# GpSimd's nucleus-search corrections in a graph network of four layers: fewer and merged operations per tile

## The chip, the cores and the metric

The kernel runs on one core of one Trainium2 chip. The metric is the time of one execution on the device in microseconds (us). The kernel before takes 3471.04 us, the median of three runs (3469.64 to 3474.25).

## What is computed

The reference takes x (3327 x 256) and an adjacency matrix adj (3327 x 3327) and passes them through four graph layers, each on a layer-normalised, rectified copy of x whose output is added to x. Layer 2 is the one that matters here. It runs two steps, and in each it builds an attention matrix in which every row keeps only its largest probabilities until they sum to 0.9 ("nucleus"):

```python
for s in range(STEPS):                       # STEPS = 2
    logits = (Xa @ W1) @ W2 @ (Xa @ W3).T
    idx = jnp.argsort(-logits, axis=1)
    csum = jnp.cumsum(jax.nn.softmax(vals, axis=1), axis=1)
    k_i = jnp.sum(csum < P_NUC, axis=1) + 1  # P_NUC = 0.9
    masked = jnp.where(keep, logits, -jnp.inf)
    A = jax.nn.softmax(masked, axis=1)
    Xf, Xb, Xa = Rf @ Xf, Rb @ Xb, A @ Xa
    Z = Z + (Xf @ U1[s] + Xb @ U2[s] + Xa @ U3[s])
```

Everything is float32.

## The kernel before

Rows are padded to 26 tiles of 128 (`NT = 26`, `NP = 3328`, `N = 3327`). The program has a front part (layer 0 and the row sums), a first plain layer, the attention part (prefix `att_`), and a last plain layer. The attention part is a software pipeline of rounds, about one round to a tile: tiles 0 to 25 are the first step, tiles 26 to 51 the second, with five rounds between them in which no new tile starts (`LAG = 5`). A tile of 128 rows passes through these stages, each a round or so behind the one before:

- **Scores.** TensorE (PE) computes the 128 x 3328 logits in four pieces (L913), ScalarE (ACT) copies each piece into `E` (L1073) and takes its sum (`musum`). VectorE (DVE) takes the row maximum (`row_max`, L1363), ACT the exponential with its row sum `Zs` (L1078).
- **Aiming, on GpSimd (POOL) and ACT.** The sorted prefix of the reference is replaced by a search for the threshold at which the mass above it is 0.9 of `Zs`. `guess(t)` works out a first threshold from the moments of the row and announces it by the semaphore `aimed[0]`. ACT makes two passes over the 3327 elements with it (L1030: a ReLU sum and a sign sum, semaphore `summed[0]`). `update(t, 0)` turns the two sums into a mass and the next threshold, a Newton step, and announces `aimed[1]`. ACT makes two more passes, and `update(t, 1)` makes a secant step and announces the start point by `bracketed`. Each of the three routines is a chain of small POOL operations on one to four values a partition, grouped in stages: `then(...)` issues its operations and waits for all of them before the next stage is issued. `update` also narrows the bracket `ends`.
- **Search, on DVE.** `find(t)` waits for `bracketed`, and takes three evaluations a tile in the first step and four in the second (`EVALS`), each a 3327-element operation (L1401) and some small ones. Then come one more pass (L1408), one or more turns of a loop of MAX8 and MATCH_REPLACE (L1422, L1432), and the masking of the row (L1448, semaphore `probs_ready`). Of these 3327-element operations L1401, L1408 and L1448 are scalar_tensor_tensor and read two tensors; L1363, L1422 and L1432 read one.
- **Use.** PE transposes the masked row in four pieces (L898), ACT copies each piece (L1069) to `PT`/`adj`, and PE multiplies them with the values (L885). In between PE multiplies the adjacency tiles (`neighbours`, L925), which is the most of its work, and makes the small dense products (L932).

The order on each engine is written out by hand. ACT in round i, for k = 0: the copies of k = 0, the exponential of the tile F, then the first pass `sums(R, 1, 0)` of the older tile R, which waits for `aimed[1]` of R; for k = 1: copies and `sums(R, 1, 1)`; for k = 2: copies and `sums(F, 0, 0)`, which waits for `aimed[0]` of F; for k = 3: copies and `sums(F, 0, 1)`. POOL in round i: (second step: sums of layer 2's outputs and layer-norm statistics), `guess(F)`, `update(R, 1)`, the rest of the statistics (`ln_tail`) or two additions of 128 x 256 (L1330, L1334, first step), then `update(F, 0)`. So what POOL announces last in one round, `aimed[1]`, is what ACT waits for near the beginning of the next.

```python
def offer(t, j):
    then(ts(negp[:, t % 2, j:j + 1], cand[:, t % 2, 0:1], -UNDER, None, ALU.mult))
    pool.sem_inc(aimed[j], 1)
```

The functions of the attention part that matter are `offer` (L1196), `prepare` (L1200), `guess` (L1207) and `update` (L1240), which the change rewrites, and on the other engines `sums` (L1020, ACT), `find` and `row_max` (DVE).

## Time and profile before

| | before |
|---|---|
| median of three runs | 3471.04 us (3469.64 to 3474.25) |
| profiled execution: its time, its span | 3468.18 us, 3466.4 us |
| granted TensorE clock, mean | 0.959 |
| PE busy | 3137.2 us (91%), 13212 matmuls |
| DVE busy | 2444.9 us (71%) |
| ACT busy | 1598.2 us (46%) |
| POOL busy | 2140.7 us (62%), 4214 instructions |

Times are microseconds from the start of the span. The clock column of the windows is the share of full speed that was granted to TensorE. The first attention step lies at about 820 to 1850 us, the second at about 1885 to 3210 us. A POOL operation is listed as busy from its start to its end, so time in which it is held up inside counts as busy. "<- issue" or "<- POOLq" behind a wait of ACT on L1030 means that no finished operation of another engine accounts for the end of the wait; those passes wait for a semaphore that POOL's queue raises after its last operation.

### The profile page before, as it was taken

Reading aid. Unit: us, or ns where it says so; the run is one execution under the profiler, and the core shown is the slowest. Engines: PE = TensorE matmul, PEld = TensorE weight load, DVE = VectorE, ACT = ScalarE, POOL = GpSimd, SP = SyncE. Lnnn points to the kernel's source line nnn. Section 1 sums busy time; section 2 is a strip of 40 time slices with the busy share of each in tenths; the row PEclk is TensorE's granted clock in tenths of the full one; section 3 lists DMA queues with packets and bytes.
Section 4 is the critical chain, followed back from the end, with each engine's and each line's share of the span. In section 5 each row is a group of like instructions: output and inputs, shape, how many; then the busy total and the mean of one; then the engine's idle time right before and its main releaser. Section 6 shows DMA issues by size and latency. Waiting matters only on the chain. (4 is left out here: it accounts for less than half of the span.)

```text
span 3466.4 us, 42065 instructions
## 1 busy us (share of the span) xinstructions
PE 3137.2 (91%) x13212; PEld 2267.5 (65%) x13212; DVE 2444.9 (71%) x3401; ACT 1598.2 (46%) x2357; POOL 2140.7 (62%) x4214
## 2 busy tenths in 40 slices
PE   4999999997899999999966698988999999996899
PEld 3888778885567777777754255544566566664788
DVE  6840123333998889888884799999988999998000
ACT  2311322225666666666753455655555555552200
POOL 2212422224788888888880677877888788786211
PEclk9999999998899999999988899999999999998899
DMA  7644344433112222222211111211222222223255
GB/s 258 239 146 146 116 156 166 165 129 87 44 54 59 60 64 58 59 60 64 58 33 63 47 57 48 63 44 55 58 82 75 73 85 82 74 83 103 92 202 173
DMA packets 140702, 327.59 MB, mean 95 GB/s; under 512 B 15456, under 2 KB 93664, under 8 KB 129248
## 3 DMA queue, kind: packets, MB, share of 16 engines
q1 hardware_dynamic: 140512, 325.30, 29.5%
q8 instruction: 90, 1.47, 0.2%
q14 instruction: 100, 0.82, 0.1%
HBM read 286.70 MB, written 38.54 MB: 94 GB/s over the span
## 5 line engine op out<-in xcount | busy, mean ns | idle before, releaser
L1030 ACT ACTIVATE junk<-E,negp 128x3327 uint8<-128x3327 f32 x208 | 637.3, 3064 | 142.8 <-issue 112.0
L1401 DVE SCALAR_TENSOR_TENSOR U<-E,trial 128x3327 f32<-128x3327 f32 x182 | 674.7, 3707 | 0.0
L925 PE MATMUL bank<-big,adj 128*128 128x512 f32 x1352 | 611.4, 603 | 11.2 <-ACT t L1056 11.2
L925 PEld LDWEIGHTS bank<-big,adj 128*128 128x128 f32 x1352 | 253.5, 193 | 333.3 <-issue 332.2
L298 PE MATMUL bank<-big,E 128*128 128x256 f32 x1664 | 364.7, 381 | 1.9 <-PEq L58 1.7
L885 PE MATMUL bank<-Hc,PT 128*128 128x256 f32 x1248 | 303.2, 395 | 66.7 <-ACT PT L1069 66.4
L298 PEld LDWEIGHTS bank<-big,E 128*128 128x128 f32 x1664 | 315.0, 191 | 48.3 <-issue 5.4
L885 PE MATMUL bank<-Hc,adj 128*128 128x256 f32 x1456 | 336.3, 383 | 9.4 <-ACT adj L1069 9.4
L1363 DVE TENSOR_REDUCE nmax<-E 128x1 f32<-128x3327 f32 x52 | 187.9, 3614 | 206.2 <-ACT E L1073 206.2
L885 PEld LDWEIGHTS bank<-Hc,PT 128*128 128x128 f32 x1248 | 244.7, 198 | 127.3 <-ACT PT L1069 77.9
L885 PEld LDWEIGHTS bank<-Hc,adj 128*128 128x128 f32 x1456 | 278.3, 192 | 72.1 <-issue 22.5
L925 PE MATMUL bank<-Hc,adj 128*128 128x256 f32 x1352 | 315.0, 384 | 1.0 <-ACT bias L1050 1.0
L925 PEld LDWEIGHTS bank<-Hc,adj 128*128 128x128 f32 x1352 | 254.2, 191 | 79.1 <-issue 48.8
L898 PE MATMUL tr<-ident,E 128*128 128x128 f32 x1352 | 191.1, 282 | 115.7 <-DVE E L1448 115.7
L1422 DVE MAX8 top<-U 128x8 f32<-128x3327 f32 x74 | 268.4, 3627 | 20.2 <-DVE mass L1410 11.7
L358 POOL TENSOR_TENSOR xn<-xt,t 128x256 f32<-128x256 f32 x52 | 37.7, 725 | 378.8 <-ACT t L329 199.8
L1432 DVE MATCH_REPLACE8 U<-mark,U 128x3336 f32<-128x3336 f32 x74 | 267.7, 3618 | 0.0
L898 PEld LDWEIGHTS tr<-ident,E 128*128 128x128 f32 x1352 | 167.2, 146 | 140.9 <-DVE E L1448 120.9
L913 PE MATMUL lg<-K,qt 64*128 64x384 f32 (+1 forms) x832 | 216.1, 598 | 33.6 <-ACT E L1073 25.3
L1069 ACT ACTIVATE adj<-tr 128x1024 f32<-128x1024 f32 x104 | 95.4, 917 | 255.4 <-PE tr L898 255.3
L1073 ACT ACTIVATE E<-lg 128x1024 f32<-128x1024 f32 x208 | 179.3, 862 | 55.0 <-PE lg L913 49.4
L1408 DVE SCALAR_TENSOR_TENSOR U<-E,ends 128x3327 f32<-128x3327 f32 x52 | 194.0, 3730 | 2.2
(248 smaller groups left out, 5729.7 us busy)
## 6 DMA issues: line engine op xcount, KB each, us to landing
adj<-adjT SPq DMA_DIRECT2D x131, 448.0 KB, 3.4
E<-adjT SPq DMA_DIRECT2D x32, 1664.0 KB, 6.9
adj<-adjT SPq DMA_DIRECT2D x104, 384.0 KB, 3.3
adj<-adjT SPq DMA_DIRECT2D x20, 1664.0 KB, 6.9
E<-adjT SPq DMA_DIRECT2D x26, 1216.0 KB, 5.7
xt<-xin SPq DMA_DIRECT2D x52, 128.0 KB, 5.6
xt<-x_d SPq DMA_DIRECT2D x52, 128.0 KB, 5.3
xo_d<-xo SPq DMA_DIRECT2D x26, 256.0 KB, 3.7
```

The source lines that it names most:

```text
L298: last = nc.tensor.matmul(acc[par][:, 0:D], bufs[par][:, j], rhs[:, j], start=(j == j0), stop=(j == NT - 1))
L885: last = mm(axp[:, 0:D], PT[k % 2][:, h, i * P:(i + 1) * P], Hc[:, j], start=(k == 0 and h == 0 and i == 0), stop=(k == SLOTS - 1 and h == ...
L898: last = nc.tensor.transpose(tr[:, h, i * P:(i + 1) * P], E[:, t % DEPTH, c0:c0 + P], ident[:])
L913: last = mm(lg[:, h, 0:w], qt[rows, t % 2], K2[rows, c0:c0 + w], start=True, stop=True)
L925: last = mm(agg[:, 0:w], adj[:, SPAN * (k % 2) + j - AGG[k]], rhs[:, j], start=(j == 0), stop=False)
L1030: go(junk[:, 0:N], E[:, t % DEPTH, 0:N], func, bias=negp[:, t % 2, j:j + 1], scale=1.0, accum_out=acc_[:, t % 2, j:j + 1]).then_inc(summed ...
L1073: go(halves(E[:, L % DEPTH])[:, :, c0:c0 + w], lg[:, :, 0:w], ACT.Copy, accum_out=musum[:, L % 2, k:k + 1]).then_inc(lg_copied, 1)
L1363: V_.tensor_reduce(nmax[:, t % DEPTH:t % DEPTH + 1], E[:, t % DEPTH, 0:N], axis=AX_X, op=ALU.max, negate=True).then_inc(max_ready, 1)
L1401: V_.scalar_tensor_tensor(out=U[:, 0:N], in0=e, scalar=point, in1=e, op0=ALU.is_ge, op1=ALU.mult, accum_out=found))
L1408: V_.scalar_tensor_tensor(out=U[:, 0:N], in0=e, scalar=hi[:, 0:1], in1=e, op0=ALU.is_lt, op1=ALU.mult, accum_out=sc[:, 5:6]))
L1422: rthen(V_.memset(U[:, N:NPAD], 0.0), V_.max(top8[:], U[:, 0:N]))
L1432: V_.match_replace(U[:], mark[:], U[:], MARKED).then_inc(rnd, 1)
```

## The change

All of it is in the three POOL routines and the two helpers that they call.

- `guess`: one operation (L1224) goes, its constant is folded into L1226, which becomes a tensor_scalar with a pointer operand. The three targets of the row (`tgt`, its negative, and `below`) are written by one 3-element tensor_tensor with constants instead of three operations in two stages; `below` is now tgt x (1 - 2^-22) instead of tgt x (1 - 2^-24), up to rounding. The secant terms (L1204, L1205) are no longer made in `guess`, and the pair of sums (L1203, now `aims`) runs beside `ends2` and the slope.
- `update(t, 0)`: the complement of the flag (`took[0]`, `took[2]`) is compared directly, beside the flag. The upper clip moves into the product before it at both places, and the lower clip and the negated threshold are made side by side from the same value. The secant terms are made here, for the second point.
- `update(t, 1)`: the same, and the slope is no longer stored: its factors are multiplied with the gap, in two stages fewer.
- Three constants are added to `known`, `trial2` grows from 5 to 7 columns.

POOL's stream has 4202 instructions in the program before and 3890 after, which is 6 fewer for each of the 52 tiles. No other engine's instructions change in kind or number.

```diff
--- before.py
+++ after.py
@@ -42,7 +42,7 @@
 LATE = 7
 FIRST = 7
 SPAN = 7
-POINT, GAP, GOAL, MASS, BELOW = 0, 1, 2, 3, 4
+POINT, GAP, GOAL, MASS, BELOW, NEG = 0, 1, 2, 3, 4, 6
 
 
 @contextmanager
@@ -655,7 +655,7 @@
             over = ab("over", [P, 2, 2])
             sign = ab("sign", [P, 2, POINTS])
             negp = ab("negp", [P, 2, POINTS])
-            known = ab("known", [P, 8])
+            known = ab("known", [P, 11])
             outset = ab("outset", [P, 2, 2, 2])
             ga = ab("ga", [P, 2, 20])
             up = ab("up", [P, 2, 24])
@@ -663,7 +663,7 @@
             took = ab("took", [P, 3])
             parts = ab("parts", [P, 2, 2, 2])
             ends2 = ab("ends2", [P, DEPTH, 2, 2])
-            trial2 = ab("trial2", [P, DEPTH, 5])
+            trial2 = ab("trial2", [P, DEPTH, 7])
             side = ab("side", [P, 2, 2], I32)
             sc = ab("sc", [P, 8])
             top8 = ab("top8", [P, TOP])
@@ -1171,7 +1171,8 @@
                         G_ = nc.gpsimd
                         tt = G_.tensor_tensor
                         ts = G_.tensor_scalar
-                        KNOWN = (1.0 / ROOT, -1.0, 0.5, float(np.e), AIM[0], STEER[0], AIM[1], STEER[1])
+                        KNOWN = (1.0 / ROOT, -1.0, 0.5, float(np.e), AIM[0], STEER[0], AIM[1], STEER[1],
+                                 P_NUC, P_NUC * (1 - 2.0 ** -22), -P_NUC)
                         values = [(known[:, i:i + 1], value) for i, value in enumerate(KNOWN)]
                         for h, scaled, fixed in ((0, 1 - P_NUC, 0.0), (1, -P_NUC, 1.5)):
                             values += [(outset[:, 0, h, 0:1], 0.0), (outset[:, 0, h, 1:2], scaled),
@@ -1193,23 +1194,16 @@
                             pool.sem_clear(step_done)
                             n[0] = 0
 
-                        def offer(t, j):
-                            then(ts(negp[:, t % 2, j:j + 1], cand[:, t % 2, 0:1], -UNDER, None, ALU.mult))
-                            pool.sem_inc(aimed[j], 1)
-
-                        def prepare(t):
+                        def aims(t):
                             q, step = t % 2, t // NT
-                            p = cand[:, q, 0:1]
-                            then(ts(up[:, q, 0:2], known[:, 4 + 2 * step:6 + 2 * step], p, ga[:, q, 12:13], ALU.mult, ALU.add),
-                                 ts(up[:, q, 3:4], p, p, RIDGE[step] ** 2, ALU.mult, ALU.mult))
-                            then(tt(up[:, q, 4:5], up[:, q, 3:4], ga[:, q, 11:12], ALU.mult))
+                            return ts(up[:, q, 0:2], known[:, 4 + 2 * step:6 + 2 * step], cand[:, q, 0:1],
+                                      trial2[:, t % DEPTH, NEG:NEG + 1], ALU.mult, ALU.add)
 
                         def guess(t):
                             q, d, step = t % 2, t % DEPTH, t // NT
                             ga_ = lambda a: ga[:, q, a:a + 1]
                             restart()
                             z, nm = Zs[:, d:d + 1], nmax[:, d:d + 1]
-                            tgt, below = (trial2[:, d, a:a + 1] for a in (GOAL, BELOW))
                             p = cand[:, q, 0:1]
                             pool.wait_ge(exp_done, t + 1)
                             if t >= DEPTH:
@@ -1220,23 +1214,21 @@
                                  ts(ga_(4), ga_(2), ROOT, -ROOT - math.log(N), ALU.mult, ALU.add))
                             then(ts(ga_(5), ga_(3), 1.0 / N, nm, ALU.mult, ALU.add))
                             then(tt(ga_(6), ga_(4), ga_(5), ALU.subtract))
-                            then(ts(ga_(7), ga_(6), 2.0, 0.01, ALU.mult, ALU.add),
-                                 ts(ga_(8), ga_(5), 1.0, -SHIFT[step], ALU.mult, ALU.add))
+                            then(ts(ga_(7), ga_(6), 2.0, 0.01, ALU.mult, ALU.add))
                             then(tt(ga_(9), ga_(7), half, ALU.pow),
-                                 tt(ga_(10), ga_(8), ga_(7), ALU.add))
+                                 ts(ga_(10), ga_(7), -SHIFT[step], ga_(5), ALU.add, ALU.add))
                             then(ts(ga_(13), ga_(9), -QUANTILE, ga_(10), ALU.mult, ALU.add))
                             then(ts(ga_(14), ga_(13), -0.001, -36.0, ALU.min, ALU.max))
                             then(tt(p, e_, ga_(14), ALU.pow))
-                            offer(t, 0)
+                            then(ts(negp[:, q, 0:1], p, -UNDER, None, ALU.mult))
+                            pool.sem_inc(aimed[0], 1)
                             shape4 = lambda ap: ap.rearrange("p a b -> p (a b)")
                             then(tt(shape4(parts[:, 0]), z.to_broadcast([P, 4]), shape4(outset[:, 0]), ALU.mult),
-                                 ts(tgt, z, P_NUC, None, ALU.mult),
-                                 ts(ga_(12), z, -P_NUC, None, ALU.mult),
+                                 tt(trial2[:, d, GOAL:NEG + 1:2], z.to_broadcast([P, 3]), known[:, 8:11], ALU.mult),
                                  tt(ga_(15), z, minus, ALU.pow))
                             then(tt(ends2[:, d], parts[:, 0], outset[:, 1], ALU.add),
-                                 ts(below, tgt, 1 - 2.0 ** -24, None, ALU.mult),
+                                 aims(t),
                                  ts(ga_(11), ga_(15), ga_(9), 1.0 / DENSITY, ALU.mult, ALU.mult))
-                            prepare(t)
 
                         def update(t, j):
                             q, d, step = t % 2, t % DEPTH, t // NT
@@ -1251,31 +1243,37 @@
                             pool.wait_ge(summed[j], PASSES[j] * (t + 1))
                             then(ts(count, sign[:, q, j:j + 1], 0.5, N / 2, ALU.mult, ALU.add))
                             then(ts(mass_, count, p, over[:, q, j:j + 1], ALU.mult, ALU.add))
-                            then(ts(cand[:, q, 1:3], up[:, q, 0:2], mass_, None, ALU.add),
-                                 ts(took[:, 1:2], mass_, tgt, None, ALU.is_ge))
-                            if j > 0:
-                                then(tt(up_(16), mass_, up_(7 + j), ALU.subtract))
+                            if j == 0:
+                                then(ts(cand[:, q, 1:3], up[:, q, 0:2], mass_, None, ALU.add),
+                                     ts(took[:, 1:2], mass_, tgt, None, ALU.is_ge),
+                                     ts(took[:, 0:3:2], mass_.to_broadcast([P, 2]), tgt, None, ALU.is_lt))
+                                then(ts(up_(21), slip, slope, STRIDE, ALU.mult, ALU.min))
+                            else:
+                                then(ts(cand[:, q, 1:3], up[:, q, 0:2], mass_, None, ALU.add),
+                                     tt(up_(16), up_(7 + j), mass_, ALU.subtract),
+                                     ts(took[:, 1:2], mass_, tgt, None, ALU.is_ge),
+                                     ts(took[:, 0:3:2], mass_.to_broadcast([P, 2]), tgt, None, ALU.is_lt))
                                 then(ts(up_(17), up_(16), up_(16), up_(3), ALU.mult, ALU.add),
-                                     tt(up_(18), up_(16), up_(20), ALU.mult))
+                                     ts(up_(18), up_(16), up_(20), up_(4), ALU.mult, ALU.add))
                                 then(tt(up_(19), up_(17), minus, ALU.pow),
-                                     tt(up_(18), up_(4), up_(18), ALU.subtract))
-                                then(tt(slope, up_(18), up_(19), ALU.mult))
-                            then(tt(up_(21), slip, slope, ALU.mult),
-                                 ts(took[:, 0:3:2], took[:, 1:2].to_broadcast([P, 2]), -1.0, 1.0, ALU.mult, ALU.add))
+                                     tt(up_(22), up_(18), slip, ALU.mult))
+                                then(ts(up_(21), up_(22), up_(19), STRIDE, ALU.mult, ALU.min))
                             wide = lambda ap: ap.unsqueeze(2).to_broadcast([P, 2, 2])
-                            then(ts(up_(20), up_(21), STRIDE, -STRIDE, ALU.min, ALU.max),
+                            then(ts(up_(20), up_(21), -STRIDE, None, ALU.max),
                                  tt(parts[:, 0], ends, wide(took[:, 0:2]), ALU.mult),
                                  tt(parts[:, 1], cand[:, q, 0:2].unsqueeze(1).to_broadcast([P, 2, 2]),
                                     wide(took[:, 1:3]), ALU.mult))
                             then(tt(up_(22), e_, up_(20), ALU.pow),
                                  tt(ends, parts[:, 0], parts[:, 1], ALU.add))
-                            then(tt(up_(23), up_(22), p, ALU.mult))
+                            then(ts(up_(23), up_(22), p, hi, ALU.mult, ALU.min))
                             if j < POINTS - 1:
-                                then(ts(p, up_(23), hi, lo, ALU.min, ALU.max))
-                                offer(t, j + 1)
-                                prepare(t)
+                                then(ts(negp[:, q, j + 1:j + 2], up_(23), lo, -UNDER, ALU.max, ALU.mult),
+                                     ts(p, up_(23), lo, None, ALU.max))
+                                pool.sem_inc(aimed[j + 1], 1)
+                                then(aims(t), ts(up_(3), p, p, RIDGE[step] ** 2, ALU.mult, ALU.mult))
+                                then(tt(up_(4), up_(3), slope, ALU.mult))
                             else:
-                                then(ts(point, up_(23), hi, lo, ALU.min, ALU.max))
+                                then(ts(point, up_(23), lo, None, ALU.max))
                                 pool.sem_inc(bracketed, 1)
 
                         def ln_tail(st, done, sums_, b):
```

The order on POOL at two places of the first step. The end of `guess` for one tile and the begin of the routine behind it, before (`Zs` is the row sum, `ga` and `up` scratch, `trial` holds the targets):

```order
L1232 TENSOR_TENSOR parts<-Zs,outset 128x4
L1233 TENSOR_SCALAR trial<-Zs 128x1
L1234 TENSOR_SCALAR ga<-Zs 128x1
L1235 TENSOR_TENSOR ga<-Zs,known 128x1
L1236 TENSOR_TENSOR ends<-parts,outset 128x4
L1237 TENSOR_SCALAR trial<-trial 128x1
L1238 TENSOR_SCALAR ga<-ga 128x1
L1203 TENSOR_SCALAR up<-known,cand,ga 128x2
L1204 TENSOR_SCALAR up<-cand 128x1
L1205 TENSOR_TENSOR up<-up,ga 128x1
```

and the same place in the changed kernel:

```order
L1226 TENSOR_TENSOR parts<-Zs,outset 128x4
L1227 TENSOR_TENSOR trial<-Zs,known 128x3
L1228 TENSOR_TENSOR ga<-Zs,known 128x1
L1229 TENSOR_TENSOR ends<-parts,outset 128x4
L1199 TENSOR_SCALAR up<-known,cand,trial 128x2
L1231 TENSOR_SCALAR ga<-ga 128x1
```

Ten operations in four stages have become six in two. The second place is `update(t, 0)` from the flag to the threshold that ACT waits for, before:

```order
L1255 TENSOR_SCALAR took<-up,trial 128x1
L1263 TENSOR_TENSOR up<-cand,ga 128x1
L1264 TENSOR_SCALAR took<-took 128x2
L1266 TENSOR_SCALAR up<-up 128x1
L1267 TENSOR_TENSOR parts<-ends,took 128x4
L1268 TENSOR_TENSOR parts<-cand,took 128x4
L1270 TENSOR_TENSOR up<-known,up 128x1
L1271 TENSOR_TENSOR ends<-parts 128x4
L1272 TENSOR_TENSOR up<-up,cand 128x1
L1274 TENSOR_SCALAR cand<-up,ends 128x1
L1197 TENSOR_SCALAR negp<-cand 128x1
```

and after:

```order
L1248 TENSOR_SCALAR took<-up,trial 128x1
L1249 TENSOR_SCALAR took<-up,trial 128x2
L1250 TENSOR_SCALAR up<-cand,ga 128x1
L1262 TENSOR_SCALAR up<-up 128x1
L1263 TENSOR_TENSOR parts<-ends,took 128x4
L1264 TENSOR_TENSOR parts<-cand,took 128x4
L1266 TENSOR_TENSOR up<-known,up 128x1
L1267 TENSOR_TENSOR ends<-parts 128x4
L1268 TENSOR_SCALAR up<-up,cand,ends 128x1
L1270 TENSOR_SCALAR negp<-up,ends 128x1
L1271 TENSOR_SCALAR cand<-up,ends 128x1
```

The number is the same, but L1249 now stands before the stage of L1250, and L1270 and L1271 are one stage instead of two.

## Rows read from the trace of the kernel before

**Rows 1.** Windows, four rounds: length; PE, PEld, DVE, ACT, POOL busy; clock; DMA:

```profile
1242.40:1282.90 40.50, 38.53 (x174) 28.78 (x173) 34.39 (x50) 26.17 (x31) 35.15 (x66) 0.96 0.20 58
1282.90:1319.40 36.50, 36.50 (x173) 27.66 (x172) 34.76 (x57) 26.18 (x31) 30.35 (x63) 1.00 0.22 64
...
1395.00:1439.50 44.50, 39.15 (x173) 29.27 (x172) 36.08 (x53) 26.17 (x31) 37.61 (x74) 0.92 0.19 52
...
1553.80:1592.80 39.00, 36.79 (x173) 27.57 (x173) 34.25 (x50) 25.95 (x31) 34.10 (x63) 1.00 0.21 59
```

**Rows 2.** Waits from 1006 to 1748 us (us in total, times, longest):

```profile
ACT junk L1030 <- issue: 86.6, 14, 9.0
...
PE bank L885 <- ACT PT L1069: 35.3, 14, 5.4
...
POOL up L1252 <- ACT junk L1030: 4.5, 5, 1.6
```

**Rows 3.** The timeline of one round, 1549 to 1570 us (start, duration, operation):

```profile
1549.65 3.62 DVE L1363 TENSOR_REDUCE nmax<-E 128x1 f32<-128x3327 f32 x1 [3.26 <-ACT E L1073]
1552.40 0.19 ACT L1030 ACTIVATION_READ_ACCUMULATOR junk<-E,negp 128x1 f32 x1
1553.37 3.68 DVE L1401 SCALAR_TENSOR_TENSOR U<-E,trial 128x3327 f32<-128x3327 f32 x1
1553.39 4.26 POOL L1334 TENSOR_TENSOR adj<-t,Hc 128x256 f32<-128x256 f32 x1
1557.92 0.19 POOL L1252 TENSOR_SCALAR up<-sign 128x1 f32<-128x1 f32 x1 [0.27 <-POOL adj L1334]
1559.06 3.68 DVE L1401 SCALAR_TENSOR_TENSOR U<-E,trial 128x3327 f32<-128x3327 f32 x1
1559.32 3.46 POOL L1263 TENSOR_TENSOR up<-cand,ga 128x1 f32<-128x1 f32 x1
1564.39 3.68 DVE L1401 SCALAR_TENSOR_TENSOR U<-E,trial 128x3327 f32<-128x3327 f32 x1
1564.42 3.69 POOL L1272 TENSOR_TENSOR up<-up,cand 128x1 f32<-128x1 f32 x1
1568.64 0.25 POOL L1197 TENSOR_SCALAR negp<-cand 128x1 f32<-128x1 f32 x1
1569.03 3.07 ACT L1030 ACTIVATE junk<-E,negp 128x3327 uint8<-128x3327 f32 x1 [5.87 <-issue]
1569.11 3.40 POOL L1203 TENSOR_SCALAR up<-known,cand,ga 128x2 f32<-128x2 f32 x1 [0.22 <-POOL negp L1197]
```

**Rows 4.** The same round's end, POOL and DVE:

```profile
1581.44 3.67 POOL L1205 TENSOR_TENSOR up<-up,ga 128x1 f32<-128x1 f32 x1
1581.45 3.60 DVE L1448 SCALAR_TENSOR_TENSOR E<-U,E 128x3327 f32<-128x3327 f32 x1
```

**Rows 5.** POOL's groups from 1006 to 1748 us (busy, mean ns of one | idle before):

```profile
L1224 POOL TENSOR_SCALAR ga<-ga 128x1 f32<-128x1 f32 x19 | 3.6, 191 | 1.6
L1233 POOL TENSOR_SCALAR trial<-Zs 128x1 f32<-128x1 f32 x19 | 3.9, 208 | 1.6
L1238 POOL TENSOR_SCALAR ga<-ga 128x1 f32<-128x1 f32 x19 | 4.9, 260 | 2.0
L1258 POOL TENSOR_SCALAR up<-up 128x1 f32<-128x1 f32 x19 | 6.4, 334 | 2.1
```

**Rows 6.** Waits from 1748 to 1885 us, the end of the first step:

```profile
PE bank L885 <- ACT PT L1069: 24.9, 4, 14.9
...
DVE sc L1399 <- POOLq L1279: 6.6, 2, 6.2
```

**Rows 7.** The second step: waits 1950 to 2480 us and 2400 to 2530 us, window 2524.7 to 3067.8 us:

```profile
PE tr L898 <- DVE E L1448: 74.4, 7, 26.3
...
PE bank L925 <- ACT t L1056: 8.6, 1, 8.6
...
2524.70:3067.80 543.10, 538.66 (x2003) 333.06 (x2002) 508.62 (x754) 311.55 (x429) 446.29 (x839) 1.00 0.27 79
```

## Prediction, written before the changed kernel ran

> **What bounds the kernel now.** I read the busy shares first, then the windows round by round, then who waits for whom, and last the timeline of one round. POOL is busy 62% of the span and PE 91%, so by the shares a change on POOL alone should be worth nothing. The windows say otherwise for the first attention step. A round in which PE never idles takes 36.5 us; the other rounds take 39.0, 40.5 and 44.5 us, and PE idles 2.0 to 5.4 us of each [rows 1]. The waits name the cause: PE waits 14 times, 35.3 us in all, for the copy L1069 on ACT; ACT, which works in order, was itself held 14 times, 86.6 us in all, before its pass L1030, by nothing that has a row, and that is the semaphore `aimed[1]` from POOL's queue. POOL waits for ACT only 4.5 us in the same 742 us [rows 2]. So in this step POOL's chain is the loop that sets the round, about 39.0 us against PE's 36.5.
>
> The timeline shows why 60 operations a tile fill 39 us. POOL's L1334, which is one addition, starts 0.02 us behind DVE's L1401 and lasts until that has ended. L1263 and L1272 do the same behind the next two L1401, and L1203 is held 3.4 us by L1408 [rows 3]; L1205 lasts the 3.6 us of L1448 [rows 4]. Beside L1363 POOL runs on. So in each tile five 3.6 to 3.7 us operations of DVE hold POOL up, with one operation caught in each, and POOL works only in what is left: some 1.6 us between two L1401, the time beside L1363, and that beside L1422 and L1432. The caught operations last 3.4 to 4.3 us, where small ones that run free last 0.19 to 0.33 [rows 3, 5].
>
> The second step is different. From 2525 to 3068 us PE is busy 538.7 of 543.1 us, so nothing on POOL can help there. Before it, from 1950 to 2480 us, PE waits 74.4 us for L1448, the end of DVE's own search, which is bound by DVE's passes; one wait of 8.6 us at about 2480 is for ACT behind POOL's statistics [rows 7].
>
> **The change, part by part**, as free-running POOL time for one tile. A tensor_tensor or a tensor_scalar with constants costs 0.19 us, with one pointer 0.26, with two 0.33 [rows 5], and a stage's end about 0.1 more.
> - `guess` loses L1224 (0.19), L1233 and L1234 (0.21 each) for one 3-element operation (0.2), L1237 (0.21), L1204 (0.26) and L1205 (0.19); L1226 gets a pointer (+0.07). That is 1.27 - 0.27 = 1.0 us, and two stages less, 1.2 us. `aimed[0]` comes only 0.1 us sooner after the start of `guess`.
> - `update(t, 1)` loses one operation and two stages, but four of the rest become operations with pointers. The durations come out even, the stages give 0.2 us.
> - `update(t, 0)` keeps its 17 operations. It gains the second flag, wider clips and the secant terms' place; it loses one stage. I take 0, with bounds of 0.3 us either way (one operation with pointers).
> - Three memsets once: nothing. DVE, ACT and PE keep their instructions; `trial2`'s wider rows change no size.
> Together 1.4 us of some 22 us free-running POOL work in a 39 us round.
>
> **What a round becomes.** I carry the timeline of [rows 3] over to PE's own pace and count from the start of L1363. PE stops being delayed if the wait of ACT is short enough: ACT waited 5.87 us there [rows 3] and PE idled 2.2 in that round (39.00 less 36.79) [rows 1], so 3.7 us are covered by PE's other work. `aimed[1]` may come up to 17.2 us after L1363 starts; it came at 19.2. DVE keeps its pace: L1401 at 3.7, 9.4 and 14.7 us, the first gap being 0.4 us longer than the second because L1334 was in flight.
> - Before, `guess` ends just as L1448 starts, so L1205 is caught (L1205 at 1581.44) [rows 4], `update(t, 1)` starts after it, the two additions run into L1401, and `update(t, 0)` starts at 8.3 us, in the gap behind it. Its fourteen operations to `aimed[1]` then need two more gaps, and L1272 misses the third L1401 by 0.03 us [rows 3].
> - After, `guess` is done 1.2 us sooner, so three or four operations of `update(t, 1)` pass before L1448. By the stage costs above `bracketed` then comes at about 1 us instead of 2.9, the additions end at 2.5, and `update(t, 0)` can start at 3.1, as soon as ACT's pass is read (1552.59) [rows 3]. Two stages pass before the first L1401; from its end at 7.4 the flags take to 8.0, the step to 8.3, the bracket's parts to 8.9; the power falls on the second L1401 and ends by 13.2; product, clip and offer need 1.0 to 1.2 us more, so `aimed[1]` comes at about 14.4. The third L1401 starts at 14.4. Either it is passed, or the offer is caught and comes at 18.3.
> - If it is passed, ACT waits under 1 us and PE does not wait. POOL's `update(t, 1)` of the next tile ends again at about 1 us of the next round, so the state holds itself up.
>
> **The sum.** First step, 1006 to 1748 us: of 35.3 us I let one long wait of 5 stay, -30. Two of the rounds with gaps show a granted clock of 0.96 and 0.92 and 38.5 and 39.2 us busy, where rounds without a gap have 1.00 and 36.5 [rows 1]; with the gaps most of that goes too, -3. End of the step: PE's 24.9 us and DVE's 6.6 us of waits are the latency of the last tiles [rows 6]; POOL gets there earlier within its round, -3, from bounds of 0 and -7. Second step: the 8.6 us wait may fall by one caught operation (3.6), or others may be caught instead; -1, from bounds of -7 and +6. Sum -37 us of the profiled execution's 3468.2, 3431; the median of the runs stands 2.9 above that execution, so 3434. I set 3436 for the likeliest case, since the long waits of the transition (44.5 us round) may come twice.
>
> A rule of the Trainium skill bears on this, and can be left out of what stands above. SBUF — State Buffer, section "Who interferes with whom", says that a VectorE instruction with two SBUF inputs contends with GpSimd's reads, that the later one blocks fully, and that issue order decides. By that rule the caught operations cost the rest of the pass, and a chain that is a little shorter can gain a whole pass of 3.7 us or nothing; a shared bandwidth would give only 1.4 us a round. The rows agree with the rule; it also says that a reduction never contends, as beside L1363.
>
> **The rivals.**
> - *Throughput only.* The offer stays behind the third L1401 in most rounds, since two operations now stand in its stage and both must be done. Then 1.4 us less work is worth at most 1.0 to 1.4 us in each of 14 gapped rounds, and 2 to 3 in the long ones: 14 x 1.2 = 17, with 3 for the rest -20, 3448 in the profile, 3451 in the median. For it: the margin at 14.4 us is nil by my estimates. Against it: a caught offer gives POOL a longer round (37.7 us), and with that a head start in the next.
> - *The gain is taken by DVE.* DVE's tile is 35.4 us from the start of L1363 to the end of L1448 [rows 3, 4], PE's 36.5, and a tile with another turn of the loop of L1422 and L1432 takes longer. If PE's gaps become waits for L1448, half of the 30 stays: 3449.
> - *Nothing.* The waits of ACT are of another origin than POOL's chain length, or the second step gives it all back: 3468 to 3474. Little speaks for it, as POOL itself waits only 4.5 us.
> - *Slower.* The pair of flags with pointers before the Newton step, and the two-operation offer, put `update(t, 0)` one pass of DVE further back: the chain starts a stage before an L1401 rather than behind it, so that five stages instead of four lie in each gap. Then a round is like that of 44.5 us with its gap of 5.4 us [rows 1], +3.4 us on each. It decides if `aimed[1]` is later than 21 us after L1363 starts, and needs more than four such rounds to outweigh the rest; with eight of the 19 it is +27 - 10 = +17, 3488.
>
> **How the numbers follow.** Forecast (gaps mostly closed) 0.55, 3420 to 3446. Throughput only 0.2, gain taken by DVE 0.12, both 3443 to 3458. Nothing 0.07. Slower 0.06. The range 3420 to 3459 leaves out the last two and a little of the first. A measurement of this kernel can tell 0.2%, about 7 us, from no change: the first three cases are faster by more than that, 0.87; of "nothing" all is within, 0.07; slower 0.06.
>
> **What would show it.** In the profile after: 312 POOL instructions fewer; the wait of PE on L1069's copies between 1006 us and the end of the first step under 10 us; rounds of 36.5 us; the wait of ACT before L1030 mostly under 1 us; `update(t, 0)` starting before the first L1401 and its offer ending before the third; the first step over 30 to 40 us earlier. From 2525 us on the rounds stay at 49.3 us (543.1 over eleven), and the second step's length stays within 6 us of before. The forecast is wrong if ACT's wait is still over 4 us in most rounds, if PE waits for L1448 instead, or if the second step is longer by what the first gives.

## The result, and the profile after

The changed kernel is slower. Its median is 3511.02 us (3477.27 to 3512.76, 13 runs) beside 3471.68 us (3468.77 to 3474.26, 13 runs) before: a ratio of 1.0092, 95% interval 1.007 to 1.0114. The forecast was 3436 us, the range 3420 to 3459. Its runs don't scatter about one value as those of before do: most lie at 3510 to 3513, others at 3477, 3496 and 3502. The profiled execution is one of 3477.27 us, so its profile shows 9.1 us of a loss of 39.

| | before | after, the execution of 3477 us |
|---|---|---|
| span | 3466.4 us | 3475.5 us |
| POOL busy, instructions | 2140.7 us, 4214 | 2146.1 us, 3905 |
| first step, 19 rounds | 1006.2 to 1747.6 us | 1009.5 to 1752.4 us |
| the next two stretches of PE's rhythm (end of the step) | 210.5 us | 212.0 us |
| from there to the end | 1508.3 us | 1511.1 us |

Of these 9.1 us only 1.5 lie in the 19 rounds, 3.3 ahead of them, 1.5 at the end of the step and 2.8 behind it. POOL has 309 operations fewer and is no less busy. The waits from 1006 to 1748 us, in the columns of [rows 2]:

```profile
ACT junk L1030 <- issue: 95.8, 18, 11.7
DVE nmax L1361 <- ACT E L1073: 62.9, 15, 9.9
...
PE bank L885 <- ACT PT L1069: 37.4, 15, 8.0
...
POOL up L1244 <- ACT junk L1030: 19.8, 4, 5.7
```

PE's wait was to fall from 35.3 us to under 10; it is 37.4, and ACT waits 18 times instead of 14. Four windows of rounds, in the columns of [rows 1]:

```profile
1208.60:1246.80 38.20, 36.85 (x174) 27.61 (x173) 33.88 (x50) 26.00 (x32) 33.96 (x57) 1.00 0.22 61
1246.80:1285.00 38.20, 36.85 (x174) 27.64 (x173) 33.86 (x50) 26.00 (x32) 33.96 (x57) 1.00 0.22 61
1398.00:1445.20 47.20, 39.18 (x174) 29.26 (x173) 36.12 (x51) 26.28 (x32) 38.49 (x69) 0.89 0.17 50
1445.20:1481.70 36.50, 36.50 (x174) 27.63 (x173) 33.80 (x50) 26.14 (x32) 31.18 (x51) 1.00 0.22 63
```

The steady round did get shorter, 38.2 us instead of 39.0. But three rounds take 45 to 47 us, each beside one of 36.5; before there were two of 44.5. One steady round, 1207 to 1232 us, against [rows 3]:

```profile
1208.32 3.62 DVE L1361 TENSOR_REDUCE nmax<-E 128x1 f32<-128x3327 f32 x1 [3.25 <-ACT E L1073]
...
1212.05 3.68 DVE L1399 SCALAR_TENSOR_TENSOR U<-E,trial 128x3327 f32<-128x3327 f32 x1
1217.38 3.68 DVE L1399 SCALAR_TENSOR_TENSOR U<-E,trial 128x3327 f32<-128x3327 f32 x1
1222.66 3.68 DVE L1399 SCALAR_TENSOR_TENSOR U<-E,trial 128x3327 f32<-128x3327 f32 x1
```

```profile
1210.92 0.73 POOL L1332 TENSOR_TENSOR adj<-t,Hc 128x256 f32<-128x256 f32 x1
1211.93 0.19 POOL L1244 TENSOR_SCALAR up<-sign 128x1 f32<-128x1 f32 x1 [0.28 <-POOL adj L1332]
1212.22 3.72 POOL L1245 TENSOR_SCALAR up<-up,cand,over 128x1 f32<-128x1 f32 x1
1216.04 0.30 POOL L1247 TENSOR_SCALAR cand<-up 128x2 f32<-128x2 f32 x1
...
1217.53 3.58 POOL L1263 TENSOR_TENSOR parts<-ends,took 128x4 f32<-128x4 f32 x1
...
1222.18 0.38 POOL L1268 TENSOR_SCALAR up<-up,cand,ends 128x1 f32<-128x1 f32 x1
1222.65 3.77 POOL L1270 TENSOR_SCALAR negp<-up,ends 128x1 f32<-128x1 f32 x1
1226.40 0.31 POOL L1271 TENSOR_SCALAR cand<-up,ends 128x1 f32<-128x1 f32 x1
```

(U is the tile that L1399 writes; "caught" means held until a pass of DVE has ended.) As forecast, the two additions end before the first pass over U (L1332 at 1211.65), but `update(t, 0)` starts 3.6 us after L1361's start and not 3.1. The offer L1270 starts 0.01 us ahead of the third pass, is caught, and comes at 18.1 us after L1361's start instead of 14.4. The second step did what was forecast: from 1950 to 2480 us PE waits 73.1 us for L1446 (before 74.4), and the 543 us window is as full.

```profile
PE tr L898 <- DVE E L1446: 73.1, 7, 26.2
...
2531.00:3074.00 543.00, 538.10 (x2002) 332.78 (x2001) 507.71 (x757) 309.96 (x430) 452.73 (x770) 1.00 0.27 79
```

### The profile page after: what moved, and what is told of

The parts are those of the page before. It is cut to its first block and busy times, and to the rows that moved or that the text cites. A ratio compares the mean times of both kernels' runs of the same rounds, so it can differ in the third digit from the quotient of the medians.

```text
span 3475.5 us, 41756 instructions
## 1 busy us (share of the span) xinstructions
PE 3144.0 (90%) x13212; PEld 2273.9 (65%) x13212; DVE 2440.9 (70%) x3401; ACT 1598.5 (46%) x2357; POOL 2146.1 (62%) x3905
## 5 line engine op out<-in xcount | busy, mean ns | idle before, releaser
L1399 DVE SCALAR_TENSOR_TENSOR U<-E,trial 128x3327 f32<-128x3327 f32 x182 | 672.5, 3695 | 0.0
L1361 DVE TENSOR_REDUCE nmax<-E 128x1 f32<-128x3327 f32 x52 | 188.0, 3615 | 217.0 <-ACT E L1073 217.0
L1406 DVE SCALAR_TENSOR_TENSOR U<-E,ends 128x3327 f32<-128x3327 f32 x52 | 193.1, 3714 | 2.2
```

Of the source, the lines that this page charges most:

```text
L1361: V_.tensor_reduce(nmax[:, t % DEPTH:t % DEPTH + 1], E[:, t % DEPTH, 0:N], axis=AX_X, op=ALU.max, negate=True).then_inc(max_ready, 1)
L1399: V_.scalar_tensor_tensor(out=U[:, 0:N], in0=e, scalar=point, in1=e, op0=ALU.is_ge, op1=ALU.mult, accum_out=found))
L1406: V_.scalar_tensor_tensor(out=U[:, 0:N], in0=e, scalar=hi[:, 0:1], in1=e, op0=ALU.is_lt, op1=ALU.mult, accum_out=sc[:, 5:6]))
```

## The experiments

Each kernel was timed beside the kernel before on the same chip, whose medians were 3467.7 to 3470.4 us. "Offer" is the end of `negp` for the second candidate, timed from the start of DVE's row maximum (in the changed text the announcement waits for L1271 too, 0.3 us more, or a whole pass where L1271 is caught); "passes" are the three over U (L1401, after: L1399) and the one behind them (L1408, after: L1406).

**The parts of the change.** First the changed kernel again (e1), then its `guess` in the old kernel (e2: the hunks of the diff up to `update`, with `then(aims(t), ts(up_(3), ...))` in place of `prepare(t)`), its `update` with the old `guess` (e3), and the changed kernel with the second flag made from the first (e4):

```diff
-                                     ts(took[:, 1:2], mass_, tgt, None, ALU.is_ge),
-                                     ts(took[:, 0:3:2], mass_.to_broadcast([P, 2]), tgt, None, ALU.is_lt))
-                                then(ts(up_(21), slip, slope, STRIDE, ALU.mult, ALU.min))
+                                     ts(took[:, 1:2], mass_, tgt, None, ALU.is_ge))
+                                then(ts(up_(21), slip, slope, STRIDE, ALU.mult, ALU.min),
+                                     ts(took[:, 0:3:2], took[:, 1:2].to_broadcast([P, 2]), -1.0, 1.0, ALU.mult, ALU.add))
```

> The changed kernel once more, for a profile of an execution at its usual time (its profiled execution took 3477 us, its median is 3511). Theory A (pass alignment): the rounds of the first step fall into one of two patterns, a steady one of 38.2 us with the offer caught behind the third L1399, and pairs of 45 and 36.5 us in which a chain lags one whole pass of DVE; the usual execution has at least ten pairs' worth of rounds of 45 us where the profiled one had four, and the first step takes all of the 34 us. Theory B (fixed price of the edits): all rounds are equally longer than 38.8 us, or the 34 us lie in the second step.

> Only the edits in guess (19 operations for 24), update as before but for the secant terms that both kernels make for the second point. Theory A: the step is set by where update(t, 0) starts against DVE's passes; with guess 1.2 us shorter and the old update, the offer lands behind the second or third pass, time anywhere from 3430 to 3515 and possibly of two kinds; halves need not add up. Theory B: guess only removes work, so it is faster than before by 10 to 25 us (3447 to 3461), and the loss of the change lies in update.

> Only the edits in update, guess as before with its 24 operations. Theory A: the offer comes 0 to 0.3 us later or sooner than before; before it was caught by 0.03 us, so little changes unless a pass is crossed: 3465 to 3475, or one jump. Theory B: the wide flags and the two-operation offer cost 0.3 us on the path in every round of the first step and lose alignment: 3490 to 3530, more than the whole change.

> The changed kernel with the second flag made as before, from the first, in the stage of the Newton step of update(t, 0) (0.19 us with constants instead of 0.30 with a pointer). Theory A: in the steady pattern the offer missed the third L1399 by 0.01 us, and 0.1 us less on the path lets it pass, so that the wait of PE on L1069 goes to zero in those rounds: under 3460 if the pattern of 45 us rounds is also left, at least 10 us under the changed kernel otherwise. Theory B: the flag is one of several costs: 3 to 8 us less than the changed kernel, 3503 to 3508.

Measured: e1 3478.14 us (3476.12 to 3509.42, 10 runs; ratio 1.0041, 1.0021 to 1.006), e2 **3436.59** (3435.27 to 3437.95; ratio 0.9902, 0.9886 to 0.9919), e3 **3517.95** (3514.85 to 3518.98; 1.0135, 1.0118 to 1.0152), e4 3477.59 (3476.49 to 3480.2, 9 runs). So `guess` alone gives the gain that was forecast for the whole, and `update` alone costs 48 us. The changed kernel itself lost 39 us in the first batch of runs and 8 in this one; its quick runs, two of 13 there, are six of ten here. Why is not shown, so a version of it can be judged against it only within one batch. Of e2 the waits from 1006 to 1748 us and two rounds:

```profile
ACT junk L1030 <- issue: 54.8, 10, 7.1
...
PE bank L885 <- ACT PT L1069: 24.5, 9, 8.6
```

```profile
1464.70:1501.20 36.50, 36.50 (x174) 27.63 (x173) 33.73 (x50) 26.19 (x31) 32.27 (x56) 1.00 0.22 64
1501.20:1539.40 38.20, 36.77 (x173) 27.58 (x172) 33.77 (x50) 25.97 (x31) 33.56 (x60) 1.00 0.21 61
```

Its rounds alternate, the offer coming at 14.4 us in one and at 18.5 in the next. In e3 they alternate between 36.5 and 45.4 to 46 us, with offers at 14.2 and 23.8. e4, whose flag is about 0.1 us cheaper, has e1's median and none of its scatter; at least 10 us less was expected. In its steady rounds the 0.1 us is lost at once: L1263 is caught by the second pass as before, the same operations follow behind it, and L1270 again starts 0.01 us ahead of the third.

**One update at a time, and a dose.** e5 has the new text for `update(t, 0)` alone, e6 for `update(t, 1)` alone. e7 has nothing of the change, but one unused operation:

```diff
                             then(ts(mass_, count, p, over[:, q, j:j + 1], ALU.mult, ALU.add))
+                            if j == 0:
+                                then(ts(up_(12), mass_, 0.5, 1.0, ALU.mult, ALU.add))
```

> The kernel before with the change's text for update(t, 0) alone (two flags with pointers, the step bounded from above in its multiply, product with the upper clip, offer and point in one stage, the secant terms behind the offer); guess and update(t, 1) as before. Theory A (pass alignment): what matters is where update(t, 0) stands in DVE's gaps. Its fourteen-odd operations to the offer were measured 0.33 us longer than before when none was caught, and the offer needs 0.3 more; that should be enough to push a further operation into a pass in every second round, pairs of 36.5 and 45 us as in the version with both updates, 3505 to 3520. Theory B (each edit costs its own duration, whatever the alignment): 19 rounds by 0.6 us is at most 12 us, 3475 to 3483.

> The kernel before with the change's text for update(t, 1) alone; guess and update(t, 0) as before. Measured free-running it is 0.25 us longer. Theory A (pass alignment): it delays the two additions and so the start of update(t, 0) by one quarter of a microsecond, which only counts if the chain of update(t, 0) has no slack left at its third L1401; before it missed that pass by 0.03 us, so most rounds can get no worse by it, 3468 to 3480; if it alone gives the pairs of 45 and 36.5 us, update(t, 1) is the culprit and the time is over 3500. Theory B (own duration): 19 rounds by 0.25 us, 3475.

> The kernel before with one more stage of one operation with constants (0.19 us and a stage's end, 0.28 us together) in update(t, 0), behind its mass; the value is not used. Nothing of the change is in it. Theory A (pass alignment): the same pairs of 36.5 and 45 us as with the change's updates appear from a third of a microsecond of any work, and the time is 3500 to 3520. Theory B (own duration): 19 rounds by 0.28 us, 3475 to 3477. If it stays at 3470 to 3480 the loss of the change's updates is not a matter of their length before the offer.

Measured: e5 3517.75 us (1.0139, 1.0122 to 1.0155), e6 3467.95 (0.9993, 0.9984 to 1.0003; 10 runs), e7 **3514.78** (1.0127, 1.011 to 1.0144). An operation of 0.19 us, which ought to cost 5 us in 19 rounds, costs 45; a quarter of a microsecond in `update(t, 1)` costs nothing. The loss of e3 is that of the new `update(t, 0)` alone. e7's windows:

```profile
1095.80:1132.40 36.60, 36.60 (x174) 27.70 (x174) 33.58 (x49) 26.19 (x31) 32.20 (x60) 1.00 0.22 64
1132.40:1177.70 45.30, 38.57 (x173) 28.87 (x172) 34.93 (x51) 26.20 (x31) 36.36 (x68) 0.92 0.18 51
```

This speaks for pass alignment against a price by duration, and the loss needs no property of the new operations. The new `guess` with only one of the new updates was not run.

**Attempts at the better side, and the dose in the other versions.** e8 is e2 with `update(F, 0)` moved ahead of the two additions (L1330, L1334). e9 and e10 put e7's operation into the changed kernel and into e2. e11 is e2 with the second flag, both bracket products and the bracket's sum behind the offer, so the second candidate is clipped to the old bracket. e12 is one more profiled execution of the changed kernel.

> The kernel before with the change's guess (3436.6 us before) and with POOL's two additions of 128x256 halves moved behind update(t, 0), so that update(t, 0) may start as soon as ACT's first pass is read. Theory A (pass alignment): every second round had its offer caught at 18.5 us after the start of DVE's row maximum; with the additions out of the way update(t, 0) starts 1 to 2 us sooner, one operation fewer stands before the first L1401, the offer passes before the third L1401 at about 14.4 in nearly all rounds, and rounds are 36.5 us: 12 to 17 us less than 3436.6, 3420 to 3426. Against it: whoever waits for the additions (PE's transposes of the next activations) gets them 14 us later; if that is on the path, 3440 or more. Theory B: the order of equal work changes nothing, 3436.

> The changed kernel with the same unused 0.19 us operation as a stage of its own in update(t, 0). Theory A (pass alignment): the changed kernel stands on an edge; in its steady rounds of 38.2 us the offer started 0.01 us ahead of the third pass over U and was caught, coming at 18.1 us after the start of DVE's row maximum. With 0.28 us more it is past the edge, one operation further back, and every second round has its offer at about 23.5: the pattern of pairs 36.5 and 45.4 us all through the step, 3508 to 3520, in every run, where the changed kernel itself gives 3477 in some runs and 3511 in others. Theory B (own duration): 3478 and 19 times 0.28 = 3483.

> The kernel before with the change's guess (3436.6 us before) and with the same unused operation in update(t, 0). Theory A (pass alignment): the offer, which passed ahead of the third pass over U in every second round (14.4 us) and was caught in the others (18.5), is caught in all; rounds of 38.1 us, and perhaps some pairs with 45: 3460 to 3480, about what the changed kernel gives in its quicker runs. So the loss of the change's updates on top of its guess is this edge. Theory B (own duration): 3442.

> The kernel before with the change's guess, and in update(t, 0) the opposite of the added stage: the second flag, the two bracket products and the bracket's sum (four operations, some 0.6 us) come behind the offer. That alters the computation in one point: the second candidate is clipped to the bracket as it was before this update, no longer to the new one. The work in all is the same but for one copy more. Theory A (pass alignment): after the second pass over U some 1.0 us of chain is left up to the offer, and the gap is 1.6 us, so the offer passes ahead of the third pass in every round, comes at about 14.3, ACT waits no more, and nearly all rounds of the step take 36.5 us: 3415 to 3428. Theory B (own duration): the work is not less, 3437 or a little more.

Measured: e8 3435.77 us (0.9897, 0.9881 to 0.9914), no different from e2, where 3420 to 3426 was expected. e9 **3478.75** (3472.81 to 3493.99), where 3508 to 3520 was expected. e10 3458.05 (0.9966, 0.9953 to 0.9979; expected 3460 to 3480), e11 **3445.93** (0.9929, 0.9916 to 0.9943), 9 us slower than e2 where 10 to 20 us less was expected. e12's execution was again one of 3477 us. So 0.28 us costs 45 us in the kernel before and 21 in e2, and a path to the offer that is 0.6 us shorter can lose. e9's median is e1's, but the changed kernel was not timed in e9's batch; its profile shows why it need not lose: the second pass catches one operation earlier, and the offer still comes at 18.2 us. In e11 the offer did pass ahead of the third pass in two rounds of three (14.6 and 13.5 us), later in the step in one of two, but the other round had begun with an addition caught in the first pass, the offer's last operation L1259 fell 0.16 us behind the third, and it came at 19.2. In e2 no addition is caught in its steady rounds: the work moved behind the offer comes ahead of the additions of the next round.

**How fine the edge is.** e13, e14 and e15 read one constant from SBUF, the same value, in the changed kernel, the kernel before and e2; that operation takes 0.26 instead of 0.19 us. e16 is e2 again.

```diff
-                            then(ts(count, sign[:, q, j:j + 1], 0.5, N / 2, ALU.mult, ALU.add))
+                            then(ts(count, sign[:, q, j:j + 1], known[:, 2:3] if j == 0 else 0.5, N / 2, ALU.mult, ALU.add))
```

> The changed kernel with one constant (0.5) of the first operation of update(t, 0) read from SBUF instead, the same value: that operation takes about 0.07 us longer and nothing else is altered. Theory A (pass alignment): the changed kernel stands on an edge of a few hundredths of a microsecond in the rounds that follow a pair of 36.5 and 45 us; pushed over it, it keeps to the pairs, each 5.5 us longer than two rounds of 38.2, and six such pairs make 3477 into 3511. So 3505 to 3515 in most runs, with pairs in the profile in place of the rounds of 38.2. If it lands on another pattern it may be 3473 to 3480, as with the whole added stage. Theory B (own duration): 19 times 0.07, 3479, and the spread of the changed kernel as before.

> The kernel before with the same 0.07 us. A stage more of 0.28 us made it 3514.8. Theory A (pass alignment): the time stands on steps; in the rounds of 39.0 us the bracket's sum already missed the third pass over U by 0.03 us, so 0.07 us more changes no catch there, 3468 to 3474; should one catch change, over 3490; a time between is against it. Theory B (own duration): 3471.

> The kernel before with the change's guess (3436.6 us before) and the same 0.07 us in update(t, 0): how near to an edge this version stands. Theory A (pass alignment): its good rounds have the offer at 14.4 us, right ahead of the third pass over U; if 0.07 us more makes it miss, 3450 to 3460 as with a whole stage more (3458.1), if not 3435 to 3439. Theory B (own duration): 3438.

(The operation called the bracket's sum in e14's text is the product L1272.) Measured: e13 **3508.86** us (3506.54 to 3510.16), e14 **3513.89** (1.0135, 1.0118 to 1.0152), e15 3441.92 (0.9927, 0.9911 to 0.9944), e16 3436.23 (0.991, 0.9894 to 0.9927). 0.07 us makes the kernel before 46 us slower. e15 lies between the two values expected: its rounds are those of e2 (19 take 718.2 us, e2's 718.1), and the end of the step is 5 us longer (213.2 against 207.9). The kernel before in the round of 39.2 us that follows its first pair of 44.4 and 36.5 (row maximum at 1082.94 us), with DVE's passes first and POOL's operations after:

```profile
1086.83 3.67 DVE L1401 SCALAR_TENSOR_TENSOR U<-E,trial 128x3327 f32<-128x3327 f32 x1
...
1092.52 3.68 DVE L1401 SCALAR_TENSOR_TENSOR U<-E,trial 128x3327 f32<-128x3327 f32 x1
...
1097.85 3.68 DVE L1401 SCALAR_TENSOR_TENSOR U<-E,trial 128x3327 f32<-128x3327 f32 x1
...
1102.08 3.68 DVE L1408 SCALAR_TENSOR_TENSOR U<-E,ends 128x3327 f32<-128x3327 f32 x1
```

```profile
1086.97 4.13 POOL L1334 TENSOR_TENSOR adj<-t,Hc 128x256 f32<-128x256 f32 x1
...
1092.41 0.29 POOL L1255 TENSOR_SCALAR took<-up,trial 128x1 f32<-128x1 f32 x1
1092.78 3.46 POOL L1263 TENSOR_TENSOR up<-cand,ga 128x1 f32<-128x1 f32 x1
...
1097.88 3.70 POOL L1272 TENSOR_TENSOR up<-up,cand 128x1 f32<-128x1 f32 x1
1101.69 0.33 POOL L1274 TENSOR_SCALAR cand<-up,ends 128x1 f32<-128x1 f32 x1
1102.10 0.25 POOL L1197 TENSOR_SCALAR negp<-cand 128x1 f32<-128x1 f32 x1
```

And the same place of e14 (row maximum at 1087.73 us), whose passes start at 1091.75, 1097.42, 1102.69 and 1106.89 us:

```profile
1097.42 3.67 DVE L1401 SCALAR_TENSOR_TENSOR U<-E,trial 128x3327 f32<-128x3327 f32 x1
...
1106.89 3.68 DVE L1408 SCALAR_TENSOR_TENSOR U<-E,ends 128x3327 f32<-128x3327 f32 x1
```

```profile
1091.89 4.12 POOL L1334 TENSOR_TENSOR adj<-t,Hc 128x256 f32<-128x256 f32 x1
1096.30 0.26 POOL L1252 TENSOR_SCALAR up<-sign,known 128x1 f32<-128x1 f32 x1 [0.29 <-POOL adj L1334]
...
1097.40 3.78 POOL L1255 TENSOR_SCALAR took<-up,trial 128x1 f32<-128x1 f32 x1
...
1102.84 3.59 POOL L1271 TENSOR_TENSOR ends<-parts 128x4 f32<-128x4 f32 x1
...
1106.82 3.79 POOL L1274 TENSOR_SCALAR cand<-up,ends 128x1 f32<-128x1 f32 x1
1110.69 0.25 POOL L1197 TENSOR_SCALAR negp<-cand 128x1 f32<-128x1 f32 x1
```

Before, L1255 started 0.11 us ahead of the second pass and got through, the clip L1274 fitted ahead of L1408, and the offer L1197 got by it too. With 0.07 us more L1255 starts 0.02 us ahead and is caught; each later catch then falls on an earlier operation, and the clip is caught by the fourth pass too. The offer comes at 23.2 us instead of 19.4, one pass later. e14's text had looked for the edge at the third pass; it lay at the second. In both kernels the round shown begins with an addition caught by the first pass, behind a round of 36.5 us. The kernel before gets away with 39.2 us and goes over to its rounds of about 39.0; e14's takes 45, the next is one of 36.5 again, and behind it an addition is caught again. A pair takes 81.7 us (e14: 36.5 and 45.2) where two rounds of 39.0 take 78. The clock does its part, as e14's long round shows:

```profile
1137.00:1173.40 36.40, 36.40 (x173) 27.55 (x172) 33.63 (x50) 26.19 (x31) 32.05 (x59) 1.00 0.21 63
1173.40:1218.60 45.20, 38.98 (x173) 29.13 (x173) 34.47 (x51) 26.19 (x31) 35.88 (x66) 0.92 0.18 52
```

Behind a gap of 6 us the granted clock is 0.92 in the mean, a mixture of the levels 2.4 and 1.2 GHz, and the same matmuls take 39.0 us instead of 36.5.

**The last link.** In e13's profile the point was ready and not announced:

```profile
1182.15 3.87 POOL L1268 TENSOR_SCALAR up<-up,cand,ends 128x1 f32<-128x1 f32 x1
1186.11 0.30 POOL L1270 TENSOR_SCALAR negp<-up,ends 128x1 f32<-128x1 f32 x1
1186.38 3.73 POOL L1271 TENSOR_SCALAR cand<-up,ends 128x1 f32<-128x1 f32 x1
```

e17 (on e13) and e18 (on the changed kernel) announce behind `negp` alone:

```diff
-                                then(ts(negp[:, q, j + 1:j + 2], up_(23), lo, -UNDER, ALU.max, ALU.mult),
-                                     ts(p, up_(23), lo, None, ALU.max))
+                                then(ts(negp[:, q, j + 1:j + 2], up_(23), lo, -UNDER, ALU.max, ALU.mult))
                                 pool.sem_inc(aimed[j + 1], 1)
+                                then(ts(p, up_(23), lo, None, ALU.max))
```

> The changed kernel with the 0.07 us pointer (3508.9 us), and the offer announced behind negp alone; the other operation of that stage, the new p, becomes a stage of its own behind the announcement. In the profile with the pointer, negp was done at 1186.41 us but p started at 1186.38, 0.03 us behind DVE's pass L1406, and was caught for 3.73 us, so ACT was released at 1190.2. Theory A (pass alignment): announced alone the offer is 3.8 us earlier in each of these rounds, ACT waits about 5.5 instead of 9.3, PE's gap of 5.6 us falls to about 2, and the pairs of 36.5 and 45.3 go over into others: 3465 to 3485. Theory B (own duration): one stage more behind the offer, 3509 to 3511.

> The changed kernel with the offer announced behind negp alone. Theory A (pass alignment): in its steady rounds negp itself is caught and done at 1226.42 us and p at 1226.71, so the offer gains only 0.3 us there; rounds of 37.9 us instead of 38.2, and the pairs at 1055 and 1401 us, where negp is caught by L1406 itself, stay: 3470 to 3477; the runs of 3496 and 3511 us are gone, because these hang on p being caught. Theory B (own duration): 3478 to 3480, with the spread of before.

Measured: e17 3505.86 us (1.0101, 1.0084 to 1.0118), e18 **3506.76** (3504.44 to 3512.05; 1.0102, 1.0085 to 1.0119). Both expectations missed: announcing earlier gave neither version the gain expected (e13 stood at 3508.9). Whether e18 loses against the changed kernel is open, as that was not timed in this batch: e18's runs are 28 us above e1's median and 4 under the 3511 of the first batch. Its profile shows the pattern of nine pairs. In e18 the one stage more behind the offer puts `update(t, 1)` one operation back at L1446 against the changed kernel's quick profile (L1255 is caught where it was L1256), so in every second round the addition L1332 is caught by the first pass (0.11 us behind its start) and the offer itself by L1406, at 22.8 us. ACT's and PE's waits show the nine pairs:

```profile
ACT junk L1030 <- issue: 82.9, 9, 11.6
...
PE bank L885 <- ACT PT L1069: 49.9, 9, 7.9
```

What stays open: no execution of the changed kernel at 3511 us was profiled. That it is this pattern is inferred: e13 and e18, each a small edit away, give it at 3509 and 3507 us; and a pair costs 5.4 us more than two rounds of 38.2 (e13: 36.5 and 45.3). e13 has nine rounds over 44 us and the changed kernel's profile three, and six pairs more make 32 of the 34 us between the kinds.

## Why the prediction was wrong

- **What bounds the kernel:** right. The first step hangs on POOL's chain to the offer, and the versions differ mostly by the rounds there. In e2's profile, 30.2 us shorter in all, the first step's 19 rounds are 23.3 us shorter, and the end of the step 2.6.
- **`guess` loses 1.2 us:** right, and a little more. From its first operation to the start of `update` it took 8.50 us before and 7.08 after (medians of each step from one start to the next, so where nothing is caught). With this part alone the forecast's number comes out, 3436.6 for 3436, but that is in part luck: nearly all rounds were to take 36.5 us and PE to wait under 10 us, and e2's alternate between 36.5 and 38.2, with 24.5 us of waits.
- **`update(t, 0)` at 0 and `update(t, 1)` at -0.2 us:** wrong. Free-running, from first to last operation, they grew by 0.33 and 0.25 us. In `update(t, 0)` nearly all of it lies ahead of the announcement, which now waits for L1271 too: from the first operation to the announcement 4.54 us instead of 4.18 (medians as above). The operations with two pointers or a minimum were priced from [rows 5]; by the rows of the changed kernel, 1006 to 1748 us, they cost more:

```profile
L1260 POOL TENSOR_SCALAR up<-up 128x1 f32<-128x1 f32 x20 | 6.2, 310 | 2.1
L1250 POOL TENSOR_SCALAR up<-cand,ga 128x1 f32<-128x1 f32 x19 | 5.8, 304 | 1.8
```

  L1268, with two pointers, took 0.38 us. The bound was 0.3 us either way: right in size, and then carried into the range as if its effect were of that size.
- **The offer at 14.4 us, in front of the third pass or caught:** the step that failed. With a margin of nothing against known errors of 0.3 us, "gaps mostly closed" at 0.55 had no ground. The steady round above shows it term by term: the start point comes at 1.6 us (forecast about 1; 0.45 of the 0.6 are `update(t, 1)`, 0.25 longer where 0.2 shorter was taken), the additions end at 3.3 (2.5), `update(t, 0)` starts at 3.6 (3.1) and has one stage ahead of the first pass, not two; the second pass catches the bracket's product L1263 and not the power, which ends at 13.6 (13.2). L1270 starts at 14.3 and the announcement, had nothing been caught, would have come at about 14.9, 0.5 us behind the forecast and behind the start of the third pass. And the steps of the chain were followed through one round only: which operation is caught at L1448 decides whether the additions meet the next first pass, and by that the next offer.
- **The state holds itself up:** not shown. No version repeats rounds of 36.5 us alone; in the repeating patterns there are at most two in a row (e8, e11). What does repeat by itself is the pair of 36.5 and 45. The rounds fall into a cycle of one (the changed kernel), two (e2, e14) or three (e10), and which one is not to be read from one round.
- **The rival "slower"** named the mechanism (`update(t, 0)` one pass further back, offers later than 21 us), and its rounds came: offers at 22.8 to 23.5 us, rounds of 45 to 47. It was priced at 17 us with eight rounds and given 0.06. Versions with nine pairs lose 36 to 48 us.
- **The rival "throughput only"** is what the steady rounds of the changed kernel do: offer caught by the third pass, 0.8 us less a round. The pairs took that back.
- **The clock and the second step:** the clock fell in the long rounds as before (0.89 in that of 47.2 us). The time from the end of the first step on stayed within 3 us.
- The rule of the Trainium skill, SBUF — State Buffer, "Who interferes with whom", that the later of the two blocks fully and that issue order decides, agrees with the trace all but for the edge: L1270 started 0.01 us ahead of its pass and L1255 in e14 0.02 us ahead, and both waited for the whole of it.

## What to carry to other kernels

Where small operations of GpSimd run in the gaps between long VectorE passes and the loop closes on itself, don't price an edit by its duration: list for each pass which operation it catches and by how much the next one escaped, and if a margin is smaller than the error of the estimate, say that the outcome is open. Such a kernel can stand right at the good side of an edge: the kernel before and e2 lost 45 and 21 us by 0.28 us more, and 46 and 6 by 0.07. (The changed kernel got both doses too, but its own time differs too much from batch to batch to say what they cost.) Test each part of a change by itself and with a small dose beside it: here one part was worth -34 us and the other +48, and the forecast took both from a count of operations.

## What the runs showed of the hardware

- One constant read from SBUF, 0.07 us in one operation, moved the whole by 46 us in the kernel before (e14) and by 6 in e2 (e15 against e16).
- A POOL operation is caught by a pass over U not by its start alone. L1255 (0.29 us) started 0.11 us ahead of it and went through; the same operation 0.02 us ahead took 3.78 us. L1197 started 0.02 us behind L1408 and still took 0.25, while L1271 in e13, 0.03 us behind L1406, took 3.73; what separates these two is not shown. Counted over both steps of all twenty traces, of the operations under 0.6 us that by their usual length would have ended at most 0.1 us behind the start of such a pass none was held; of those that would have ended 0.3 us behind it or later nine in ten were.
- The same program can take clearly different times from run to run: the changed kernel 3477, 3496 or 3511 us (33 us apart in e1's ten runs), while e4, 0.1 us away and timed in the same batch, stayed within 4 us in nine. That it settles in different cycles is inferred.
- The best version, with e8 beside it, is e2: 3436.6 and 3436.2 us in two batches of runs, 1% under the kernel before.
